# First cross-attention of a two-layer decoder: three runs of turned blocks instead of two, and the plain tails moved into the double banks

## The reference, cut to what matters

```python
q_r = jnp.einsum('bshq,hqr->bhsr', q_big, W_qr)
k_r = jnp.einsum('bld,hdr->bhlr', kv_r, W_kr)
scores = jnp.einsum('bhsr,bhlr->bhsl', q_r, k_r)
attn = jax.nn.softmax(scores, axis=-1)
ctx_c = jnp.einsum('bhsl,bld->bhsd', attn, kv_r)
```

## Time and profile before

| | |
|---|---|
| median of 3 runs | 1365.95 us (1364.26 to 1366.72) |
| span of the profiled execution, its own time | 1379.6 us |
| mean granted TensorE clock in it | 0.954 |
| PE busy, share of the span | 1272.7 us, 92% |
| DVE, ACT, POOL busy | 868.2, 634.6, 824.0 us |
| exponentials of the stage (L1286), 416 | 213.3 us, mean 599 ns |
| plain reductions (L1622), 192 | 225.8 us, mean 1218 ns |
| tail reductions (L1630), 32 | 13.7 us, mean 428 ns |
| GpSimd's additions (L2080), 160 | 379.7 us, mean 2373 ns |

### The profile page before, as it was taken

How to read it: one execution, slowest core, us unless ns; L and a number is a source line. 1 busy time by engine, 2 the same in 40 slices (tenths; PEclk the granted TensorE clock), 3 DMA queues, 4 the chain that set the end, 5 groups by cost and what they waited for, 6 DMA issues and landing times.

```text
span 1379.6 us, 20358 instructions
## 1 busy us (share of the span) xinstructions
PE 1272.7 (92%) x7123; PEld 826.8 (60%) x7123; DVE 868.2 (63%) x1490; ACT 634.6 (46%) x1687; POOL 824.0 (60%) x748
## 2 busy tenths in 40 slices
PE   7999997999999999999999758998999999989792
PEld 4865554666666666666668643445776874556582
DVE  4756666677777777778865636675666123664443
ACT  3731123445554455544551416887665115872151
POOL 1267005799999999999993445887444004560444
PEclk9999997999999999999999888999999997998897
DMA  9501111000000000000005620000000105200263
GB/s 261 134 9 32 37 31 27 9 8 9 9 11 10 9 9 9 10 11 9 9 5 176 195 65 2 1 1 1 1 1 1 27 1 155 63 1 32 69 142 118
DMA packets 66172, 58.91 MB, mean 43 GB/s; under 512 B 19424, under 2 KB 62968, under 8 KB 65560
## 3 DMA queue, kind: packets, MB, share of 16 engines
q1 hardware_dynamic: 62952, 49.09, 12.7%
q0 software_dynamic: 3120, 8.52, 2.6%
HBM read 40.69 MB, written 8.52 MB: 36 GB/s over the span
## 4 chain that ended last, share of the span: by engine, by line
PE 79%; DVE 6%; ACT 5%; POOL 4%; issue 4%; DMA 1%; DVEq 0%; SPq 0%; POOLq 0%; ACTq 0%
PE PS L515 73%; PE PS L523 5%; ACT s_sc L1402 2%; POOL a_m L2137 2%; POOL a_m L2131 2%; DVE s_mx L1859 1%; ACT a_m L1356 1%; DVE pm L1622 1%; DVE HN L1504 0%; PE PS L729 0%; DMA f_xg<-token_rows,f_ids 0%; POOL s_sc L2152 0%; PE PS L685 0%; POOL f_xg L2119 0%; PE PS L623 0%
## 5 line engine op out<-in xcount | busy, mean ns | idle before, releaser
L2080 POOL TENSOR_TENSOR PWS<-PWS 128x1024 f32<-128x1024 f32 x160 | 379.7, 2373 | 45.1 <-ACT PWS L1286 25.8
L1622 DVE TENSOR_REDUCE pm<-PS 128x2 f32<-128x1024 f32 x192 | 225.8, 1218 | 69.3 <-PE PS L515 68.7
L1286 ACT ACTIVATE PWS<-PS 128x512 f32<-128x512 f32 (+1 forms) x416 | 213.3, 599 | 78.4 <-PE PS L515 78.2
L515 PE MATMUL PS<-PWS,KVR 128*64 128x256 f32 (+1 forms) x1664 | 185.8, 380 | 0.0
L515 PE MATMUL PS<-QALL,KH 128*128 128x512 f32 (+1 forms) x416 | 182.6, 439 | 0.9 <-DVE QM L1646 0.9
L515 PE MATMUL PS<-QM,KL 68*128 68x512 f32 (+1 forms) x416 | 167.3, 402 | 0.0
L2152 POOL TENSOR_SCALAR s_sc<-s_sc,s_ri 128x128 f32<-128x128 f32 (+1 forms) x256 | 104.5, 429 | 98.9 <-DVE s_ri L1866 98.9
L515 PEld LDWEIGHTS PS<-PWS,KVR 128*64 128x64 f32 (+1 forms) x1664 | 121.4, 137 | 59.0 <-issue 0.9
L515 PEld LDWEIGHTS PS<-QALL,KH 128*128 128x128 f32 (+1 forms) x416 | 77.9, 187 | 76.9 <-ACT PWS L1286 57.4
L1402 ACT ACTIVATE s_sc<-PS,s_nb 128x128 f32<-128x128 f32 (+1 forms) x256 | 104.5, 433 | 3.9 <-DVE s_nb L1862 3.9
L1859 DVE TENSOR_REDUCE s_mx<-PS 128x2 f32<-128x512 f32 (+2 forms) x112 | 65.7, 611 | 50.1 <-PE PS L515 50.0
(11 more groups left out here) (328 smaller groups left out, 2518.3 us busy)
## 6 DMA issues: line engine op xcount, KB each, us to landing
QALL<-qlo SPq DMA_DIRECT2D x32, 128.0 KB, 2.4
QM<-QALL SPq DMA_DIRECT2D x64, 64.0 KB, 2.0
f_w<-in_L_ffn_w_dram SPq DMA_DIRECT2D x2, 2048.0 KB
tile_results<-e_y SPq DMA_DIRECT2D x31, 128.0 KB
a_nat<-in_L_attn_w_qkv_dram SPq DMA_DIRECT2D x1, 3072.0 KB, 13.0
x_wq<-in_L_xattn_Wq_dram SPq DMA_DIRECT2D x1, 2048.0 KB, 10.4
x_wo<-in_L_xattn_Wo_dram SPq DMA_DIRECT2D x2, 1024.0 KB, 6.9
a_wo<-in_L_attn_w_o_dram SPq DMA_DIRECT2D x1, 2048.0 KB, 17.5
```

The source lines that it names most:

```text
L515: return nc.tensor.matmul(o, a, b, start=start, stop=stop, **kw)
L1286: nc.scalar.activation(PW[c][0:rows, j * HALF:(j + 1) * HALF], st_bank("block", LT * u + lt)[0:rows, :], ACT.Exp).then_inc(p_ready, 1)
L1622: V.tensor_reduce(pm[u % 2][:, :, i // 3, i % 3], src, AX, ALU.max).then_inc(nat_read, 1)
L2080: G.tensor_tensor(ACC[:, :], PW[0][:, :] if i == 0 else ACC[:, :], PW[i + 1][:, :], ALU.add).then_inc(acc_step, 1)
```

## The change

PLAINS becomes 7 and the tail is the fifth plain step of its unit (index TAIL = 4). It uses the double bank of its turn: for each query half one matmul per head, one in the upper and one in the lower 64 rows, with the high parts of the query alone. It waits and is counted like every plain step, and the tail's own semaphores and its place in the ring of three go. The middle has three plain steps instead of two (tail, then the unit's last two). The turned blocks go in runs of 4, 5 and 4: the first before the middle, the second between middle and late, the third behind late, so that the turn of the maxima follows the third run. VectorE reduces in the new order. The diff, without the removed semaphores and the trivial lines:

```diff
-        PLAINS = 6
+        PLAINS = 7
+        TAIL = 4
-        FRONT, BACK = range(0, 6), range(6, LT)
+        RUNS = (range(0, 4), range(4, 9), range(9, LT))
...
-                    for a, z in ((4, 6), (6, 8), (8, 10))]
+                    for a, z in ((4, 7), (7, 9), (9, 11))]
+        def plain_part(n):
+            u, i = divmod(n, PLAINS)
+            return u, None if i == TAIL else i - (i > TAIL)
-        ST_ITEMS = [("tail", 0), ("maxima", 0)]
+        ST_ITEMS = [("maxima", 0)]
         for u in range(UNITS):
-            ST_ITEMS += [("block", LT * u + lt) for lt in (FRONT if u else range(LT))]
-            ST_ITEMS += [("tail", u + 1)] if u + 1 < UNITS else []
-            ST_ITEMS += [("block", LT * u + lt) for lt in (BACK if u else ())]
+            ST_ITEMS += [("block", LT * u + lt) for lt in range(LT)]
...
                 if n >= 2:
                     pe.wait_ge(nat_read, n - 1)
+                if i is None:
+                    plain_tail(n, b, p)
+                    return
...
+            def plain_tail(n, b, p):
+                if p == 0:
+                    pe.wait_ge(rows_set, 2 if b else 1)
+                    pe.wait_ge(*(kl_ready, 4 * b) if b else banks.emptied(("k", 3)))
+                for st in range(2):
+                    for h in range(2):
+                        last = mm(plain_banks(n)[:, h * 512 + st * 256:h * 512 + st * 256 + 66],
+                                  QALL[h * D:(h + 1) * D, p, b, h, st * P:(st + 1) * P],
+                                  KH[b % 2][h * D:(h + 1) * D, 3 * HALF:3 * HALF + 66])
+                last.then_inc(nat_full, 1)
...
-                ps = st_begin("tail", u)
-                for h in range(2):
-                    for st in range(2):
-                        a = h * 256 + st * P
-                        last = mm(ps[:, a:a + 66], QALL[:, p, b, h, st * P:(st + 1) * P], KH[b % 2][:, 3 * HALF:3 * HALF + 66])
-                last.then_inc(tail_full, 1)
...
             for n in range(PLAINS):
                 plain_scores(n)
-            plain_tail(0)
             turn_maxima(0)
             for u in range(UNITS):
                 middle, late, after = plains_after(u)
-                turned_scores(u, FRONT)
+                turned_scores(u, RUNS[0])
                 if u == 0:
                     for n in range(PLAINS, PLAINS + 2):
                         plain_scores(n)
-                    turned_scores(0, BACK)
+                    turned_scores(0, RUNS[1])
                     for n in range(PLAINS + 2, PLAINS + AHEAD):
                         plain_scores(n)
-                if u + 1 < UNITS:
-                    plain_tail(u + 1)
+                    turned_scores(0, RUNS[2])
                 for n in middle:
                     plain_scores(n)
                 if u > 0:
-                    turned_scores(u, BACK)
+                    turned_scores(u, RUNS[1])
                 for n in late:
                     plain_scores(n)
+                if u > 0:
+                    turned_scores(u, RUNS[2])
                 if u + 1 < UNITS:
                     turn_maxima(u + 1)
...
             def maxima(n):
...
+                if i is None:
+                    src = plain_banks(n).rearrange("p (h s c) -> p h s c", h=2, s=2)[:, :, :, 0:LREST]
+                    V.tensor_reduce(pm[u % 2][:, :, :, 3], src, AX, ALU.max).then_inc(nat_read, 1)
+                    return
```

More of the change, by code:

```diff
@@ L390, in decoder @@
         nat_read = sem("plain_scores_reduced")
-        tail_full = sem("plain_tails_filled")
-        tail_read = sem("plain_tails_reduced")
         mx_ready = sem("query_maxima_ready")
@@ L478, in st_freed @@
             return {"keys": lambda: (kl_ready, 4 * (at_[0] - 1) + at_[1] + 1), "maxima": lambda: (qm_ready, at_[0] + 1),
-                    "block": lambda: (p_ready, at_[0] + 1), "tail": lambda: (tail_read, at_[0] + 1),
+                    "block": lambda: (p_ready, at_[0] + 1),
                     "sums": lambda: (norm_done, at_[0] + 1)}[kind]()
@@ L688, in plain_scores @@
             def plain_scores(n):
-                u, i = divmod(n, PLAINS)
+                u, i = plain_part(n)
                 b, p = divmod(u, PAIRS)
@@ L705, in plain_scores @@
                 last.then_inc(nat_full, 1)
[L707 to L714, removed]
-                ps = st_begin("tail", u)
-                if p == 0 and b > 0:
-                    pe.wait_ge(rows_set, 2)
-                    pe.wait_ge(kl_ready, 4 * b)
-                for h in range(2):
-                    for st in range(2):
-                        a = h * 256 + st * P
-                        last = mm(ps[:, a:a + 66], QALL[:, p, b, h, st * P:(st + 1) * P], KH[b % 2][:, 3 * HALF:3 * HALF + 66])
-                last.then_inc(tail_full, 1)
+            def plain_tail(n, b, p):
[8 more added lines that the diff above has]
+                last.then_inc(nat_full, 1)
             def turn_maxima(u):
@@ L733, in turned_scores @@
                 b, p = divmod(u, PAIRS)
-                if blocks is FRONT:
+                if blocks[0] == 0:
                     pe.wait_ge(qh_moved[u % 2], 32 * (u // 2 + 1))
                     pe.wait_ge(qm_ready, u + 1)
+                if u == 0 and blocks[0] == 0:
+                    pe.wait_ge(*banks.emptied(("q", PAIRS - 1, 1)))
+                    pe.wait_ge(rows_set, 1)
+                    for s in range(2):
+                        pe.wait_ge(q_moved[s], 32 * PAIRS)
                 for lt in blocks:
@@ L1302, in _ @@
             for u in range(UNITS):
-                weights(u, FRONT)
-                weights(u, BACK)
+                weights(u, range(LT))
                 if keys_due(u):
@@ L1620, in maxima @@
                     dve.wait_ge(mx_ready, u - 1)
+                if i is None:
+                    src = plain_banks(n).rearrange("p (h s c) -> p h s c", h=2, s=2)[:, :, :, 0:LREST]
+                    V.tensor_reduce(pm[u % 2][:, :, :, 3], src, AX, ALU.max).then_inc(nat_read, 1)
+                    return
                 src = plain_banks(n).rearrange("p (h c) -> p h c", h=2)
                 V.tensor_reduce(pm[u % 2][:, :, i // 3, i % 3], src, AX, ALU.max).then_inc(nat_read, 1)
[L1624 to L1630, removed]
             def all_maxima(u):
                 dve.wait_ge(nat_read, PLAINS * (u + 1))
-                dve.wait_ge(tail_read, u + 1)
                 if u >= 2:
@@ L1677, in _ @@
                 maxima(n)
-            tail_maxima(0)
             all_maxima(0)
@@ L1684, in _ @@
                 middle, late, after = plains_after(u)
-                if u + 1 < UNITS:
-                    tail_maxima(u + 1)
                 for n in middle:
```

## The result

The changed kernel takes 1394.35 us (median of 4 runs, 1385.57 to 1401.99), against 1366.05 for the kernel before (4 runs, 1364.26 to 1366.72): a ratio of 1.0213, interval 1.0166 to 1.0260. Run once more beside the kernel before on one chip it took 1389.64 against 1362.39, 1.0229 (1.0173 to 1.0286). It is slower, as forecast, and by more than forecast: some 2% (the interval lies on both sides of 2%), where the forecast's 1386, range 1371 to 1397, is 1.5%.

The account below looks back on a forecast made before the run. TensorE was taken as the bound, busy throughout; 18 units at +0.68, 11 with keys at +0.77, +0.6, +0.2 and -1.6 gave +19.9 us on the 1365.95 median: 1386, range 1371 to 1397.

Parts of the forecast that it names:

- (a): First run of 4 turned blocks in a unit, up to the middle's first load: 2.16 us.
- (c): Second run, 5 turned blocks between middle and late plain steps: 2.64 us.
- (d): The two late plain steps: 0.66 us, their double banks already read during the second run.
- (b): Middle, tail and two plains: 1.40 us, including 0.52 of stall while the third plain step waits for the tail's reduction.
- (e): Third run, 4 blocks: maxima turned at 2.08 without wait, sums 0.40 later at 2.48, losing 0.20 us.
- margin of 0.08: VectorE frees the bank for the middle's second plain step 0.08 us before its load at 3.04, so no wait.
- rival 3: Tail pairs do not overlap (+0.22 per unit, 1392) or VectorE comes later in the middle (+0.3, 1395); 17%.
- Unit 0: The first unit, bound by VectorE's reductions, was to save 1.6 us, with bounds of -3 and +1.
- two full reductions less, -2.4: In the first unit, VectorE's queue after the turned blocks was to be two full reductions shorter: -2.4 us.
- 1 (GpSimd as the bound): TensorE's unit falls below 15.42 us and GpSimd's queue sets the pace: 8 us faster, 1358; 7%.
- 2 (hidden): The middle's round trip is hidden by a quicker tail fill or reduction: 15 us less than forecast, 1371; 10%.
- the chain's last term: VectorE's low part, 2.16 us, ending the chain of maximum rows, reciprocal and context scaling that took 5.45 us.

Follow-up runs that it names:

- the fourth experiment: Kernel before with three runs of turned blocks and paired tails in the ring's bank and the context's bank, outside the double banks: 1383.38 us, ratio 1.0160.
- The second experiment: Changed kernel with two runs of turned blocks (6 and 7) instead of three, paired tails kept in the double banks: 1379.58 us, ratio 1.0132.
- the doubled reduction: Changed kernel with VectorE's tail reduction made twice, the first into an unused place: 1411.95 us in a single execution.
- the third experiment: Kernel before, two runs kept, with tails paired, one head in the ring's bank, the other in the context bank's unused half: 1359.69 us, ratio 0.9972.

## Why the prediction was right, point by point

- **The bound** and the method held. A unit was to take 16.21 and takes 16.26 (with keys 16.74, measured 16.86); units 1 to 29 were to lose 12.2 + 8.5 + 0.6 = 21.3 and lose 22.8. The miss lies in the units with keys: three of the eleven took only 15.58 to 15.61 before, where the forecast had 15.97 for all, and take 16.74 to 16.76 now.
- **(a), (c), (d), the runs**: 2.16, 2.64 and 0.66 were forecast, 2.18, 2.65 and 0.67 stand in the rows.
- **(b), the round trip**: the middle was to take 1.40 and takes 1.37; without the wait 0.88, and the fourth experiment has 0.89. This was the step that decided. The second experiment has the wait without the third run, the fourth the third run without the wait, and the doubled reduction lengthens the wait and the unit alike.
- **(e), the sums behind the third run**: the sums were to come 0.40 behind the turn of the maxima and come 0.49 behind it. From that turn to the context it is 0.94 now and was 0.69, a loss of 0.25 where 0.20 was forecast. With keys the turns follow by 0.49, not 0.40, and take 0.56, not 0.53; that makes the 0.12 by which the units with keys were missed. So the mechanism was right and its size 0.05 to 0.12 too small; why the wait is that much longer I did not follow up. What the exposed load and the first wait of the third run cost beyond the sums is read from the rows; no run shows it alone.
- **VectorE** was said to have a margin of 0.08 ahead of the middle's second plain step. It has about 0.1: in all 29 units that step's load comes 0.14 to 0.16 us behind the reduction it needs, of which 0.05 is the release (in the second experiment's last five units, where the load does wait for it, it comes 0.05 behind). So rival 3's wait did not come, but by no more than the forecast said. That VectorE is idle for 2.8 to 2.9 us before the plain steps behind the context in most units without keys (0.7 to 1.0 with keys, 0.4 in the last six) adds nothing to this margin, which runs from the moment a plain step is full. One sign did not come: VectorE is not idle before the maximum rows, which start 0.13 behind the late reductions, as against 0.03 before.
- **Unit 0**: forecast -1.6, not seen. Where both openings were clocked low for 31 us they took 39.31 and 39.27. Of it, the opening plain steps lost 0.53 (from the first to unit 0's first block 10.88 before, 11.41 changed; 0.3 forecast), the blocks and plains up to the next turn of the maxima won 0.72 (19.38 to 18.66), the rest lost 0.15. The term "two full reductions less, -2.4" came nearly true: from the last block's last matmul to the turn it is 7.13 us before and 4.96 now. What the sum left out is that two plain steps which stood behind the blocks, beside VectorE's queue, now stand between them: from the first block to the last one's last matmul it is 12.25 before and 13.70 now.
- **The rivals**: 1 (GpSimd as the bound) could not come, because TensorE's unit grew; the third experiment, at a mean of 451.73 / 29 = 15.58, is still above GpSimd's 15.42. 2 (hidden) is out by 29 waits. For the tail itself the pairs bring what was hoped: four loads in a row took 0.48 up to the next plain step's load, and the two pairs take 0.22 in all 29 units; the middle without a wait lasts 0.88 to 0.93 instead of 1.16. The Trainium skill's rule on halves (TensorEngine Tiling (Array Packing), section Theoretical Speedup) gives a contraction of at most 64 up to twice the speed; here the step from 0.48 to 0.22 is a little more than that. What cost the time was the place to which the halves' results go.
- **The total**: 1386 was forecast and 1394 and 1390 are measured. Of the 8 us, 1.5 are the units and 1.6 unit 0; the other 5 lie outside the units, in executions whose mean clock is lower (0.948 to 0.963, against 0.952 to 0.968 for the kernel before), which the forecast had carried over as nothing. The mechanism and the 21.3 us for the units were no luck; that the first median lies in the range was in part. It is above the forecast's own 1379 to 1391, in the piece of the range that stood for rival 3, whose waits did not come, and of the 8 us that took it there some 5 went with the clock.

## What to carry to other kernels

A buffer pair hides a reader as long as no run of writers is longer than the pair: count the steps in a row, not the steps per period, and price the next one at fill plus read plus release, less the steps that lie between. An engine with idle time can still be the one waited for, and work that shrinks on the bound engine is worth nothing if its new place puts a round trip on that engine; here the same tails gained 3.4 us in another bank and lost 8.6 in the double banks. When an order is rewritten, look also at what the removed neighbour had covered: the two plain steps between the last block and the sums had hidden an exponential.

## What the runs showed of the hardware

VectorE's low part (L1665 before, L1663 after: two inputs and an output in SBUF, 256 columns) takes anything from 0.42 to 2.47 us in these two kernels. Its end is tied to GpSimd: it starts, in the timeline of before, during one of GpSimd's additions and ends 0.28 us after that addition,

```profile
402.95 1.29 DVE L1665 TENSOR_TENSOR CTXL<-CTX,QALL 128x256 fp32r<-128x256 f32 x1 [0.48 <-ACT QALL L1297]
```

with GpSimd's rows of the same stretch:

```profile
401.60 2.36 POOL L2080 TENSOR_TENSOR PWS<-PWS 128x1024 f32<-128x1024 f32 x1
404.04 1.35 POOL L2084 TENSOR_TENSOR WS<-PWS 128x512 f32<-128x512 f32 x1
```

The addition ends at 403.96, the low part at 404.24. In the profile of before 31 of the 32 low parts start during a GpSimd instruction and end 0.28 to 0.31 us after its end; the one that does not takes 0.43. In the changed kernel it is again 31 of 32, and the mean fell from 1.45 to 1.01 us, with the additions now standing elsewhere relative to it. The scaling before it, with one input in PSUM, takes 0.42 every time. The Trainium skill, SBUF — State Buffer, section SBUF: two separate sides, states that VectorE and GpSimd share a port pair, and that whichever starts first holds it for its whole instruction while the other blocks; it counts VectorE's operations with two SBUF inputs in, against GpSimd operations that read SBUF. These rows agree. So the duration of this instruction, read from one row, is not its own: the 2.16 that I took as the chain's last term was mostly GpSimd's addition.
